# Patch embedding of a vision tower: two more chunks of the first row of patches computed in 28 passes instead of 19

## The chip, the core and the metric

The kernel runs on one NeuronCore of a Trainium2 chip. The metric is the device time of one execution in microseconds (us). The engines are named as the profile names them: PE is TensorE (PEld is its weight load), ACT is ScalarE, DVE is VectorE, POOL is GpSimd, and SP only issues transfers.

## What is computed

The reference is one layer of a vision tower on 128 images of 3 x 224 x 224. Only its first part is touched here, but the second part waits for it:

```
# patches of 28 x 28 pixels x 3 colours, 8 rows of 8 patches in an image
patches = X.reshape(B, 3, 8, 28, 8, 28).transpose(0, 2, 4, 1, 3, 5).reshape(B, 64, 2352)
tokens  = einsum('bpi,hi->bph', patches, W) + b            # 2352 -> 128
tokens  = concatenate([class_token, tokens], axis=1) * pos_embed      # 65 tokens
h = tokens + attention(layernorm(tokens))   # gated attention with a damped moving average
h = h + experts(layernorm(h))               # 8 experts, each takes its 1024 best tokens
```

The attention runs over the 128 images at one token position, so each of the 65 positions can be worked on as soon as its own tokens are there. The experts need all positions.

## The kernel before

**Chunks.** A row of patches (8 of them, all images) is computed in eight chunks of 16 images, so there are 64 chunks, numbered n from 0. Eight of them make one row; the first row is chunks 0 to 7. A chunk is loaded by three transfers into one of three buffers (`RAW`). It has 84 partitions: 28 pixel rows x 3 colours. Each pixel column of the patch is then one pass of PE: a matmul with 84 partitions of pixels against the weights of that column, added up in PSUM. There are 28 columns (`PATCH`), which would be 28 passes.

**Shifted columns.** To save passes the last nine columns (`REST`) can be folded into the 44 partitions that are left over. POOL copies the nine columns of a chunk to a staging buffer `ST` (one of two, by n % 2; line 588, `stage_C`), and two transfers issued by POOL (line 601, `stage_w`) move the two halves of the pixel rows to partitions 84 to 125 beside the first eighteen columns. The first 18 passes then have 126 partitions, one more has 84, and the chunk takes 19 passes (`PASSES`).

**Direct chunks.** A chunk listed in `DIRECT` is not shifted. It takes 28 passes of 84 partitions: nineteen read the copy that ACT makes (line 697, into `XS`), and nine read the staging buffer `ST` itself, with weights that are kept in the tiles `G` and `XR` for a while. PE does both kinds in the same routine (`token_pass`, line 1397). POOL may refill a buffer of `ST` only when its last reader is done. For a shifted chunk that is the pair of transfers, for a direct chunk it is PE:

```
if n - 2 in DIRECT:
    pool.wait_ge(*pe_tok.done(n - 2))
else:
    pool.wait_ge(*extras[n % 2].done(shifted(n - 2)))
```

**Order of the work.** All engines run the same hand-written list of steps, `SLOT`, in which `"C 0 3"` is POOL's staging copy of a chunk (in the first iteration that of chunk 3; `"C 1 3"` is chunk 4), `"C 0 0"` to `"C 0 2"` are ACT's three copies of it, and the other letters are stages of the attention for a group of four token positions (or, for the first group, `CLS`, of the class token alone). In the first iteration the part of the list that matters here reads

```
"S b", "C 0 3", "w 0", "T a", "U b", "C 0 0", "Z b", "P b", "N a", "K 0", "X a", "E a", "C 0 1", "C 0 2", "W 0", "O b", "C 1 3", ...
```

For the class group `a`, `T` is PE's transpose of its tokens (line 1436), then ACT's copy and DVE's statistics (lines 943 and 948, tile `mvA`). `N` is POOL's reciprocal root (lines 510 and 512, tile `rsA`) and then DVE's normalised `X` (line 935). `X` is PE's transpose of it (line 1446). `V` is lines 1456 and 984; `D` and `I` are matmuls with `WmT` (lines 1471 to 1482). In the first iteration PE has the class group alone beside the tokens, and it fills up between the stages with passes: chunk 0 ahead of `T`, chunk 1 behind `T`, chunk 2 behind `X`, chunk 3 behind `V`, and so on (`FILL_CLS`). Each engine is strictly in order, so a step that waits holds all that stands behind it on its engine. When chunk 7 is done DVE adds bias and position (line 955, `tokT`), and the groups of the first row begin.

**Ahead of the first pass** DVE works out small constants (lines 913 to 931); PE, and POOL from chunk 3 on, wait for their end (`consts_done`).

Of the kernel before, what the change touches and what calls it, by code (L numbers as in the profile page):

```python
# [17 lines left out]
def begun(n):  # L18

    return not isinstance(n, int) or n >= 0  # L20
# [15 lines left out]
def vit_tower(nc, x, tok_w, tok_b, cls_token, pos_embed, proj_v_w, proj_v_b, proj_mx_w, proj_mx_b,  # L36
# [44 lines left out]
    CHUNKS = B // CHUNK  # L81
# [7 lines left out]
    with ctx:  # L89
# [278 lines left out]
        AHEAD = 3  # L368
        DIRECT = range(3, CHUNKS)

        def passes_of(n):
            return PATCH if n in DIRECT else PASSES

# [3 lines left out]
        def shifted(n):  # L377

            return len([m for m in range(n % 2, n, 2) if m not in DIRECT])

# [116 lines left out]
        def _(pool):  # L497
# [77 lines left out]
            def stage_C(n, piece):  # L575
# [5 lines left out]
                if begun(n - 2):  # L581
                    if n - 2 in DIRECT:
                        pool.wait_ge(*pe_tok.done(n - 2))
# [7 lines left out]
            def stage_w(n):  # L591

                if n in DIRECT:
                    return
# [744 lines left out]
        def _(pe):  # L1339
# [39 lines left out]
            def token_pass(p):  # L1379
# [4 lines left out]
                if t == 0:  # L1384
                    pe.wait_ge(*copied.done(n))
                    if n in DIRECT:
                        pe.wait_ge(*staged.done(n))
                    else:
                        pe.wait_ge(*extras[n % 2].done(shifted(n)))
                    if k % 4 == 0 and begun(i - 1):  # L1390
                        pe.wait_ge(*dve_K[half].done(i - 1))
                rows = slice(0, KROWS if t < 2 * REST and n not in DIRECT else ROWS)
                if t < PASSES:
# [305 lines left out]
```

## Time and profile before

| | us |
|---|---|
| median of three runs (lowest, highest) | 955.01 (953.62, 955.89) |
| profiled execution, its own time | 960.5 |
| its span in the profile | 958.4 |
| PE busy | 766.0 |
| POOL busy | 477.1 |
| DVE busy | 561.4 |
| ACT busy | 445.5 |

The span is what the profile covers from the first instruction to the last; the time of the same execution is 2.1 us longer. The durations below come from this one execution. The token passes (line 1397) end at about 554 us; what follows is the rest of the attention, the choice of tokens and the experts.

### The profile page before, as it was taken

How to read it: one execution, taken by the hardware profiler on the slowest of the kernel's cores; microseconds unless marked ns; L12 is line 12 of the kernel's file. 1: busy time of each engine (PE TensorE's matmuls, PEld its weight loads, DVE VectorE, ACT ScalarE, POOL GpSimd, SP SyncE). 2: the span in 40 equal slices, each digit the busy share in tenths (PEclk: the TensorE clock that was granted, in tenths of full speed). 3: DMA queues.
4: the chain of work that ended last, by engine and by line, in shares of the span. 5: the costliest groups of instructions: out<-in, count | busy, mean ns of one | idle time of the engine just before them, and what ended most of it. 6: DMA issues, size and time to landing. Idle time of an engine off the chain costs nothing.

```text
span 958.4 us, 13714 instructions
## 1 busy us (share of the span) xinstructions
PE 766.0 (80%) x4819; PEld 595.1 (62%) x4819; DVE 561.4 (59%) x1239; ACT 445.5 (46%) x733; POOL 477.1 (50%) x478
## 2 busy tenths in 40 slices
PE   1799999999999999999999966443167999788771
PEld 1799888878887887888888754131124554444330
DVE  1303687788788778777877865944877433321110
ACT  2553666666756666665676624210550233222220
POOL 2314554555445546455544512441103578887885
PEclk9899999999999999999999996856557899888896
DMA  9977999998898898889889210000101133433432
GB/s 225 211 174 175 214 211 207 212 205 203 198 221 193 204 219 198 195 200 216 193 202 219 76 56 22 11 12 22 11 4 24 29 63 59 64 62 65 67 40 25
DMA packets 135057, 124.71 MB, mean 130 GB/s; under 512 B 17385, under 2 KB 125793, under 8 KB 134861
## 3 DMA queue, kind: packets, MB, share of 16 engines
q1 hardware_dynamic: 113600, 91.27, 41.7%
q0 software_dynamic: 18848, 31.58, 17.4%
q10 hardware_dynamic: 2540, 0.99, 0.5%
q8 instruction: 39, 0.64, 0.3%
q14 instruction: 30, 0.24, 0.1%
HBM read 87.99 MB, written 12.98 MB: 105 GB/s over the span
## 4 chain that ended last, share of the span: by engine, by line
DVE 27%; PE 23%; POOL 22%; issue 16%; ACT 6%; DMA 3%; ACTq 1%; another core or an unknown queue 0%; SPq 0%; DVEq 0%; POOLq 0%
POOL out L641 10%; PE bank L1397 9%; POOL XS L631 6%; DVE Y L993 4%; PE bank L1503 3%; DVE stats L943 3%; DVE XR L935 3%; DVE O L935 3%; DVE QT L1067 3%; ACT XS L844 2%; POOL rsB L512 2%; ACT S L800 2%; PE bank L1488 2%; POOL rsC L512 2%; PE bank L1534 2%
## 5 line engine op out<-in xcount | busy, mean ns | idle before, releaser
L1397 PEld LDWEIGHTS bank<-XS,WT 126*128 126x128 f32 (+1 forms) x2432 | 303.6, 191 | 20.7 <-issue 20.0
L1397 PE MATMUL bank<-XS,WT 126*128 126x128 f32 (+1 forms) x2432 | 310.5, 283 | 6.1 <-issue 6.1
L697 ACT ACTIVATE XS<-XS 84x1152 f32<-84x1152 f32 (+1 forms) x192 | 184.4, 1032 | 0.0
L588 POOL COPY XS<-XS 84x1152 f32<-84x1152 f32 x64 | 91.3, 1427 | 62.9 <-PE bank L1397 32.1
L641 POOL DMA_INDIRECT out<-XS x64 | 105.4, 1647 | 27.2 <-issue 18.7
L631 POOL DMA_INDIRECT XS<-token_rows,XS x64 | 65.4, 1022 | 54.8 <-DVE XS L1270 35.9
L993 DVE TENSOR_TENSOR_SCAN Y<-qdec,XT 128x512 f32<-128x512 f32 (+1 forms) x68 | 78.3, 1173 | 2.5 <-ACT XT L733 2.5
L873 ACT ACTIVATE XS<-bank,VT 128x512 f32<-128x512 f32 x64 | 43.8, 688 | 70.4 <-PE bank L1615 70.4
L601 POOL DMA_DIRECT2D XS<-XS x118 | 66.4, 565 | 17.3 <-POOL XS L588 17.3
L1615 PE MATMUL bank<-XS 128*128 128x512 f32 x128 | 68.8, 687 | 1.1 <-ACT XS L733 0.8
L999 DVE SCALAR_TENSOR_TENSOR ET<-Y,ema_c,ET 128x512 f32<-128x512 f32 (+1 forms) x68 | 62.7, 922 | 1.8
L1625 PE MATMUL bank<-XS 128*128 128x512 f32 x128 | 57.5, 592 | 0.0
L510 POOL TENSOR_SCALAR rsA<-mvA 128x4 f32<-128x4 f32 (+1 forms) x17 | 3.9, 232 | 95.5 <-DVE mvA L948 95.5
L733 ACT ACTIVATE XS<-bank 128x512 f32<-128x512 f32 x16 | 9.6, 597 | 89.7 <-PE bank L1606 83.2
L562 POOL TENSOR_TENSOR QT<-QT,XT 128x512 f32<-128x512 f32 (+1 forms) x17 | 23.3, 1372 | 55.0 <-ACT QT L814 55.0
L1286 DVE TENSOR_SCALAR XS<-bank,VT 128x512 f32<-128x512 f32 x16 | 12.0, 750 | 63.1 <-PE bank L1625 48.5
L1615 PEld LDWEIGHTS bank<-XS 128*128 128x128 f32 x128 | 27.6, 228 | 31.7 <-issue 31.6
L935 DVE TENSOR_SCALAR XR<-O,mvC,rsC 128x128 f32<-128x128 f32 x65 | 42.5, 918 | 8.0 <-POOL rsC L512 7.9
L510 POOL TENSOR_SCALAR rsB<-mvB 128x4 f32<-128x4 f32 (+1 forms) x17 | 15.1, 889 | 60.6 <-DVE mvB L948 60.6
L955 DVE SCALAR_TENSOR_TENSOR tokT<-bank,VT 128x512 f32<-128x512 f32 x16 | 17.9, 1118 | 46.1 <-PE bank L1397 46.1
L1625 PEld LDWEIGHTS bank<-XS 128*128 128x128 f32 x128 | 24.1, 190 | 29.7 <-issue 29.5
L1054 DVE SCALAR_TENSOR_TENSOR G<-bank,VT,GT 128x512 f32<-128x512 f32 (+1 forms) x34 | 24.7, 727 | 28.2 <-PE bank L1503 27.5
(243 smaller groups left out, 1332.1 us busy)
## 6 DMA issues: line engine op xcount, KB each, us to landing
XS<-in_x SPq DMA_DIRECT2D x192, 392.0 KB
XS<-XS POOLq DMA_DIRECT2D x118, 189.0 KB, 7.5
out<-O SPq DMA_DIRECT2D x16, 256.0 KB, 9.7
token_rows<-XR SPq DMA_DIRECT2D x16, 256.0 KB, 8.6
XS<-in_L_ffn_W SPq DMA_DIRECT2D x16, 256.0 KB
XS<-in_L_tok_W SPq DMA_DIRECT2D x1, 1176.0 KB, 9.3
XS<-token_rows,XS POOLq DMA_INDIRECT x65, 3.7
out<-XS POOLq DMA_INDIRECT x64
```

Of the source, the lines that this page charges most:

```text
L588: pool.tensor_copy(ST[0:ROWS, n % 2, :, :, :].rearrange("p m j r -> p m r j"), px[:, :, :, PASSES:PATCH])\
L601: pool.dma_start(area(slice(ROWS, KROWS), k // 4, a, m0, m0 + CCOL // 2), ST[EXTRA * a:EXTRA * a + EXTRA, n % 2, :, :, :]).then_inc(extras ...
L631: pool.indirect_dma_start(out=XG[h][:, k, :], out_offset=None, in_=rows_d, in_offset=bass.IndirectOffsetOnAxis(ap=IDX[:, e, k:k + 1], axis ...
L641: pool.indirect_dma_start(out=out_flat, in_=OW[:, e % 2, k, :], in_offset=None, out_offset=bass.IndirectOffsetOnAxis(ap=IDX[:, e, k:k + 1] ...
L697: ins = act.activation(area(slice(0, ROWS), k // 4, piece, m0, m0 + CCOL // 2).rearrange("p m j r -> p m r j"), px[:, :, :, REST * piece:m ...
L873: act.activation(HT[:, h, f, :], bank[3 + f][:, :], ACT.Gelu, bias=VT[:, ds(R_B1 + FC * e + f, 1)]).then_inc(act_hid.sem, 1)
L935: last = dve.tensor_scalar(dst(t), src(t), mv[:, gr.parity, t, 0:1], rs[:, gr.parity, t:t + 1], ALU.subtract, ALU.mult)
L993: dve.tensor_tensor_scan(Y[:, h % 2, 0:n], qdec[:, h, 0:n], XT[:, p, 0:n], 0.0, ALU.mult, ALU.add)\
L999: dve.scalar_tensor_tensor(out=ET[:, gr.parity, 0:n], in0=Y[:, h % 2, 0:n], scalar=ema_c[:, h:h + 1], in1=ET[:, gr.parity, 0:n], op0=ALU.m ...
L1397: ins = pe.matmul(TOK[half][:, c0:c0 + CCOL], weights, pixels, start=(t == 0), stop=(t == passes_of(n) - 1))
L1615: pe.matmul(bank[3 + f][:, :], W1s[:, h, 128 * f:128 * f + 128], XGT[:, half, :], start=True, stop=True).then_inc(pe_hid.sem, 1)
L1625: last = pe.matmul(bank[7][:, :], W2s[:, h, f, :], HT[:, half, f, :], start=(f == 0), stop=(f == FC - 1))
```

## The change

`DIRECT`, the chunks that are not shifted, is chunks 3 to 7 before and chunks 1 to 7 with the change. Nothing else differs.

```
-        DIRECT = range(3, CHUNKS)
+        DIRECT = range(1, CHUNKS)

         def passes_of(n):
             return PATCH if n in DIRECT else PASSES
```

On PE, behind the transpose of the class tokens (L1436), the program reads as follows against before. `WT` holds the weights of the first nineteen columns, `G` and `XR` those of the last nine, and 128x128 is the shape of the result.

```order
 L1436 MATMUL bank<-ident,tokT 128x128
 L1397 MATMUL bank<-XS,WT 128x128 x19
+L1397 MATMUL bank<-XS,G 128x128 x8
+L1397 MATMUL bank<-XS,XR 128x128
 L1446 MATMUL bank<-ident,X 128x128
 L1397 MATMUL bank<-XS,WT 128x128 x19
+L1397 MATMUL bank<-XS,G 128x128 x8
+L1397 MATMUL bank<-XS,XR 128x128
 L1456 MATMUL bank<-WvT,XT 128x128 x2
 L1397 MATMUL bank<-XS,WT 128x128 x19
```

Nine passes are added ahead of `X` (chunk 1) and nine behind it (chunk 2). On POOL, from the staging copy of chunk 1 on, this stood before, with the semaphores that each waits for (`load` is a chunk's arrival, `extras` the two shifting transfers, `pe_tok` PE's last pass of a chunk, `dve_T` the statistics):

```order
L588 COPY XS<-XS 84x64x2x9 [waits load1]
L601 DMA XS<-XS 42x1152 [waits staged]
L601 DMA XS<-XS 42x1152
L588 COPY XS<-XS 84x64x2x9 [waits load2,extras0]
L601 DMA XS<-XS 42x1152 [waits staged]
L601 DMA XS<-XS 42x1152
L588 COPY XS<-XS 84x64x2x9 [waits consts_done,load0,extras1]
L510 TENSOR_SCALAR rsA<-mvA 128x1 [waits dve_T]
L512 TENSOR_TENSOR rsA<-rsA,neghalf 128x1 [waits pool_N]
```

And this stands there now, from the same copy on:

```order
L588 COPY XS<-XS 84x64x2x9 [waits load1]
L588 COPY XS<-XS 84x64x2x9 [waits load2,extras0]
L588 COPY XS<-XS 84x64x2x9 [waits consts_done,load0,pe_tok]
L510 TENSOR_SCALAR rsA<-mvA 128x1 [waits dve_T]
L512 TENSOR_TENSOR rsA<-rsA,neghalf 128x1 [waits pool_N]
L522 TENSOR_TENSOR H<-H,lnb 128x128 [waits dve_N]
L588 COPY XS<-XS 84x64x2x9 [waits load1,pe_tok]
```

Four transfers are gone. The copy of chunk 3, which stands directly ahead of the class group's reciprocal root, waits for PE's last pass of chunk 1 where it waited for the shifting of chunk 1; the next one, of chunk 4, waits for PE's last pass of chunk 2. DVE, ACT and SP have the same instructions in the same order as before.

## Rows read from the trace of the kernel before

**Rows 1.** The page: the span, and the granted clock in 40 slices

```profile
span 958.4 us, 13714 instructions
PEclk9899999999999999999999996856557899888896
```

**Rows 2.** Chain that ended last, 24 to 125 us: start, us, what

```profile
33.30 7.02 PE bank L1397 x38
...
40.43 4.55 PE bank L1397 x38
...
50.09 6.70 PE bank L1397 x56
...
57.24 6.70 PE bank L1397 x56
...
64.39 20.11 PE bank L1397 x168
...
84.52 1.12 DVE tokT L955
```

**Rows 3.** Waits of PE from 90 to 530 us: in total, times, longest

```profile
PE bank L1520 <- DVE X L1071: 5.7, 13, 0.7
...
PE bank L1534 <- ACT X L733: 0.4, 1, 0.4
```

**Rows 4.** Timeline at chunk 1: start, us, engine, line [idle before <-releaser]

```profile
40.27 4.71 PE L1397 MATMUL bank<-XS,WT 126*128 126x128 f32 x38
...
41.28 0.18 DVE L948 BATCH_NORM_AGGREGATE mvA<-stats 128x2 f32<-128x6 f32 x1
41.69 0.24 POOL L510 TENSOR_SCALAR rsA<-mvA 128x1 f32<-128x1 f32 x1 [3.62 <-DVE mvA L948]
42.01 0.59 POOL L512 TENSOR_TENSOR rsA<-rsA,neghalf 128x1 f32<-128x1 f32 x1
42.63 0.35 DVE L935 TENSOR_SCALAR X<-H,mvA,rsA 128x128 f32<-128x128 f32 x1 [1.17 <-POOL rsA L512]
...
44.82 0.27 PE L1446 MATMUL bank<-ident,X 128*128 128x128 f32 x1
```

**Rows 5.** Timeline at chunk 5, a direct one

```profile
64.22 4.70 PE L1397 MATMUL bank<-XS,WT 84*128 84x128 f32 x38
...
70.68 0.40 PE L1397 MATMUL bank<-XS,XR 84*128 84x128 f32 x2
...
71.25 1.33 POOL L588 COPY XS<-XS 84x1152 f32<-84x1152 f32 x1 [5.83 <-PE bank L1397]
```

**Rows 6.** Timeline of DVE and POOL ahead of the first pass

```profile
28.88 1.23 DVE L917 COPY qdec<-ema_t 128x2048 f32<-128x2048 f32 x1
28.92 2.34 POOL L588 COPY XS<-XS 84x1152 f32<-84x1152 f32 x1 [3.99 <-DMA XS<-in_x]
...
30.29 0.97 DVE L919 TENSOR_TENSOR ema_t<-ema_t,ema_in 128x4 f32<-128x4 f32 x1
31.30 0.16 DVE L920 TENSOR_TENSOR ema_c<-ema_t,ema_in 128x4 f32<-128x4 f32 x1
```

**Rows 7.** Timeline of PE: three transposes with PE's idle time ahead

```profile
560.60 0.68 PE L1495 MATMUL bank<-ident,S 128*128 128x128 f32 x2 [3.69 <-DVE S L1043]
...
605.73 0.44 PE L1520 MATMUL bank<-ident,X 128*128 128x128 f32 x2 [2.67 <-DVE X L1071]
...
654.47 0.66 PE L1520 MATMUL bank<-ident,X 128*128 128x128 f32 x4 [3.58 <-DVE X L1071]
```

**Rows 8.** Stretches: busy time of five engines, then PEclk, DMA share, GB/s

```profile
33.00:38.00 5.00, 4.70 (x22) 4.73 (x23) 0.14 (x2) 0.00 (x0) 1.23 (x1) 0.50 0.97 220
...
560.00:565.00 5.00, 4.13 (x22) 3.73 (x23) 2.02 (x6) 1.92 (x3) 2.04 (x2) 0.66 0.02 5
602.00:606.00 4.00, 1.33 (x7) 0.85 (x6) 3.93 (x6) 0.05 (x1) 1.42 (x1) 1.00 0.00 0
650.00:655.00 5.00, 1.42 (x7) 0.48 (x5) 1.38 (x2) 0.69 (x1) 1.26 (x1) 1.00 0.00 0
```

## The prediction, made before the changed kernel ran

> **What bounds the kernel now.** I read the page first, for the span and the clock: PE's granted clock is at 8 or 9 tenths from the second slice on to about 550 us [rows 1]. Then the chain that ended last, from 24 to 125 us. The reader is to see that from 33.30 to 84.5 us it never leaves PE: chunk 0 (38 instructions, two to a pass), chunks 1 and 2 at 4.55 us each, then the direct chunks at 6.70 us each, with only the few matmuls of the class group between; behind chunk 7 it goes to DVE, which makes the tokens for the first groups [rows 2]. So the first row of patches is a queue of passes on PE, and all that follows waits for its end. Then the waits of PE from 90 to 530 us, to see whether a later row could give back what the first one loses: there are five rows, the longest 5.7 us in 13 waits, the smallest 0.4, and none of them is for a load or for a copy of a chunk [rows 3]. From then on, too, PE or what it hands to DVE and gets back sets the time, and nothing waits for the memory. A delay of the first row arrives at the end undiminished.
>
> **The added passes.** A chunk of 19 passes, 18 of them with 126 partitions, takes 4.55 us for 38 instructions, 119.7 ns each; a direct chunk takes 6.70 us for 56 instructions with 84 partitions, 119.6 ns each [rows 2]. Time goes by the pass and not by the partitions, so nine passes more cost 6.70 - 4.55 = 2.15 us a chunk, and two chunks **4.3 us**. Neither chunk had a wait ahead of it that they could fill: each starts as the one before it ends [rows 2, 4].
>
> **The wait that moves to POOL.** The staging copy of chunk 3 now waits for PE's last pass of chunk 1, and the class group's reciprocal root stands behind it in POOL's queue; behind that come DVE's `X` and, on PE, the transpose L1446, which stands directly behind chunk 1. Before, the root ran from 41.69 to 42.60 and `X` was there at 42.98, while PE was busy with chunk 1 until 44.8: 1.8 us to spare [rows 4]. Now, step by step:
> - Chunk 1 starts at 40.27 [rows 4]. A direct chunk ends 6.86 us after its start (64.22 to 70.68 + 0.40 [rows 5]), so it ends at 47.13. POOL's copy follows 0.17 us behind such an end (71.08 to 71.25) and takes 1.33 [rows 5]: 47.30 to 48.63.
> - The two root instructions took 0.91 us from start to end (41.69 to 42.60), DVE's `X` 0.38 with its handover (to 42.98) [rows 4]: 49.54, then 49.92. With some 0.05 us to PE, by the size of the handover to DVE, the transpose starts at 49.97.
> - PE would have come to it at 44.82 + 2.15 = 46.97. So it stands idle for **3.0 us**.
>
> That is exposed to its full length, since PE is in order and chunk 2 stands behind the transpose. Half a chunk's passes left to do there would have covered it.
>
> The next such wait, of chunk 4's copy on the end of chunk 2, costs nothing: the class group's `X` is then past, and nothing that PE needs soon stands behind the copy. Chunk 2 ends at about 56.9, the copy at 58.3, and PE wants chunk 4's staged columns only after chunk 3, 6.7 us behind chunk 2 [rows 2]; the cover is some 6 us. Chunk 3's own staged columns are there at 48.6 and are wanted after 57. ACT's copies of chunks 3 to 5 stand behind ACT's copy of the class group's transpose, and so come some 5 us later; PE wants the first of them over 7 us after that transpose, one chunk and a little more, and there are two pieces of about 1 us to do. The loads that hang on these copies shift with the stream. I cost all of these at nothing.
>
> **What is taken away.** Four transfers and their issue on POOL. PE did not wait for them. There is one way in which they could matter. Ahead of the first pass DVE's chain of small operations is on the path. L919, 0.97 us, has as many elements as L920, 0.16 us, and it ends at 31.26, exactly where POOL's copy of chunk 2 ends, which itself took 2.34 us where 1.33 is usual, while L917 ran [rows 5, 6]. So the two engines hold each other up there. That copy was waiting for its load; without the shifting of chunk 1 beside it, the load may land sooner and the copy be out of the way. Bounds: 0 if the load lands as before, 0.97 - 0.16 = 0.8 us if the collision is gone. I take **0.3**, nearer the lower end, since the two transfers of chunk 1 are only a part of what is under way in that stretch beside the loads, and a copy only a little earlier would hold up L917 in its turn.
> The Trainium skill, SBUF — State Buffer, section "Who interferes with whom", says that DVE and GpSimd lock a shared pair of ports for a whole instruction and the loser waits. The equal ends at 31.26 agree with it. By that rule alone, with the copy started before L917 and done before L919, the whole 0.8 us would come back.
>
> **The clock after the wait.** PE's clock is at 1.2 GHz until 38 us and at its full 2.4 GHz when the wait comes [rows 1, 8]. A wait of 3.0 us might cost it. The trace has three like it that began at full clock. Idle for 2.67 us at 603 to 606, the clock stayed at 1.00; idle for 3.58 us to 654.47, it was at 1.00 still at 655; idle for 3.69 us to 560.60, it fell to 1.2 GHz [rows 7, 8]. In the last the mean of 0.66 over 5 us means 5 x (1 - 0.66) / 0.5 = 3.4 us at the lower level. What that costs is seen at chunk 0: 7.02 us against 4.55 for the same 38 instructions, 2.5 us lost over the 5 us and a little at 0.50 from 33 on [rows 2, 8], so 0.47 us for each us, and 3.4 us would cost 1.6. The bounds are 0 and 1.6. I take **0**, since 3.0 us lies next to 2.67 and below 3.58, which both held.
> The Trainium skill, TensorE: Matmul & The Clock Gate, section "HAM oscillation — how this bites in real kernels", warns that an array which waits between bursts falls back to its half rate and pays the way up each time. By that the sum would be the one with 1.6 in it.
>
> **Sum.** 4.3 + 3.0 - 0.3 + 0 = 7.0 us. The profiled execution would go from its own 960.5 to 967.5 (span 965.4). It was 5.5 us above the median of the runs, 955.0, so I put the same difference on the median: **962.0 us**.
>
> **The rivals.**
> - *The clock falls after the wait.* 7.0 + 1.6 = 8.6: 963.6. For it: the 3.69 us wait, and that its outcome may differ between executions. Against it: the two that held.
> - *The wait is not there*, because something lets the root through earlier, or `X` isn't needed where I think. Then 4.3 - 0.3 = 4.0: 959.0. Against it: the order on POOL and PE, which leaves no other way.
> - *Not slower: later rows give it back.* If the loads set the pace of the later rows, a longer first row would let them run ahead, and the rows after it would close up. It would need PE to wait for chunks in the later rows by more than 5.1 us in sum, to bring 7.0 under 1.9. PE's waits there add up to 16 us, but all are for results of DVE and ACT that come from PE's own earlier work [rows 3]. It would give 955 to 957.
> - *Another queue is late too*, say ACT's three copies behind the class group's transpose: one more wait of 2 to 4 us, 964 to 966. The cover counted above speaks against it.
>
> **How the numbers follow.** The forecast has a chance of 0.52, the clock's fall 0.29, the added passes alone 0.07, another late queue 0.06, and no slowdown 0.06, of which 0.02 faster. What a measurement of this kernel can tell from no change is about 0.2%, 1.9 us; its three runs lie within 2.3 us. All cases but one are beyond that bound on the slow side: slower 0.94, same 0.04, faster 0.02. The range is to hold the forecast and the clock's fall with the prologue's 0 to 0.8 us (961.5 to 963.9), and the scatter of the runs, 1.2 us to a side; that is 960.3 to 965.1, rounded outward a little toward the two neighbouring cases: 960.0 to 965.8.
>
> **What the changed profile would show.** L1397 with 36 instructions more. Behind L1436, 56 of them in one run of about 6.9 us. Then PE idle by 3 us ahead of L1446, released by DVE's `X` (L935), at about 50 us. POOL's L588 of chunk 3 released by PE at about 47, and rsA directly behind it. DVE's `tokT` for the second half at about 91.5 where it was 84.52 [rows 2]. Then the same periods as before. PEclk at 1.00 in the stretch from 47 to 57 if the clock holds, lower if the first rival has it. If L919 takes 0.16 us and the first pass starts before 33.3, the prologue gave something back. The prediction is wrong if PE goes from chunk 1 to L1446 with no idle time, or if a wait for a chunk turns up on PE between 50 and 91 us, or if the time between `tokT` and the end has changed by more than 1 us.

## The result, and the profile after

The changed kernel takes 994.43 us (993.24 to 996.05) where the one before takes 954.63 on the same chip: a ratio of 1.0417, with a 95% interval of 1.0387 to 1.0447, 39.8 us slower. The prediction was 962.0, in a range of 960.0 to 965.8. The sign was right and the size was not: some 33 us are missing from the sum.

The page of the changed kernel shows where to look. In the row of the granted clock the slices two to five, of 24.8 us each, are at 8, 5, 5 and 5 tenths where before they stood at 8 or 9 [rows 1], and PE is busy all the same:

```profile
span 993.5 us, 13782 instructions
...
PE   1699999999999999999999995725228899878771
...
PEclk9855589999999999999999998775555798889896
```

The chain that ended last (start, us, what) answers to [rows 2]:

```profile
33.39 7.44 PE bank L1397 x38
...
40.94 6.72 PE bank L1397 x56
...
50.99 11.95 PE bank L1397 x56
...
63.79 11.95 PE bank L1397 x56
...
89.39 35.85 PE bank L1397 x168
...
125.27 1.13 DVE tokT L955
```

Chunk 1 takes 6.72 us for its 28 passes, as forecast. Chunk 2, behind the wait, takes 11.95 for the same 56 instructions, and so do all chunks up to the seventh (35.85 for three). Between chunks 1 and 2 is the wait, in the timeline of the changed kernel, which answers to [rows 4, 5]:

```profile
41.80 0.18 DVE L948 BATCH_NORM_AGGREGATE mvA<-stats 128x2 f32<-128x6 f32 x1
...
47.25 0.40 PE L1397 MATMUL bank<-XS,XR 84*128 84x128 f32 x2
47.82 1.26 POOL L588 COPY XS<-XS 84x1152 f32<-84x1152 f32 x1 [16.47 <-PE bank L1397]
49.17 0.24 POOL L510 TENSOR_SCALAR rsA<-mvA 128x1 f32<-128x1 f32 x1
49.50 0.58 POOL L512 TENSOR_TENSOR rsA<-rsA,neghalf 128x1 f32<-128x1 f32 x1
50.12 0.35 DVE L935 TENSOR_SCALAR X<-H,mvA,rsA 128x128 f32<-128x128 f32 x1 [8.14 <-POOL rsA L512]
...
50.52 0.47 PE L1446 MATMUL bank<-ident,X 128*128 128x128 f32 x1 [2.87 <-DVE X L935]
```

The statistics are ready at 41.98 and the root starts at 49.17, behind the copy. PE stands idle for 2.87 us. The stretches of the changed kernel (length, then busy time of PE, PEld, DVE, ACT and POOL, the granted clock, DMA share, GB/s) show the clock at this place, in the middle of what follows, and at the start of the second row of patches:

```profile
48.00:49.00 1.00, 0.00 (x0) 0.00 (x0) 0.00 (x0) 0.00 (x0) 1.00 (x1) 1.00 0.00 0
49.00:50.00 1.00, 0.00 (x0) 0.00 (x0) 0.00 (x0) 0.00 (x0) 0.82 (x3) 0.85 0.00 0
50.00:51.00 1.00, 0.48 (x2) 0.49 (x3) 0.35 (x1) 0.00 (x0) 0.53 (x2) 0.50 0.00 0
...
100.00:125.00 25.00, 25.00 (x119) 25.00 (x118) 0.00 (x0) 0.00 (x0) 3.70 (x4) 0.50 0.50 118
...
130.00:131.00 1.00, 1.00 (x6) 1.00 (x6) 0.05 (x1) 0.00 (x0) 0.92 (x2) 0.50 0.05 14
131.00:132.00 1.00, 1.00 (x8) 1.00 (x7) 0.68 (x3) 0.00 (x0) 0.28 (x1) 0.69 0.00 0
132.00:133.00 1.00, 1.00 (x11) 1.00 (x10) 0.43 (x2) 0.00 (x0) 0.49 (x1) 1.00 0.00 0
```

The clock falls from 2.4 to 1.2 GHz at about 49.7 us, while PE is idle, and stays there until 131.6, although PE is busy from 50.5 to 125 without a break, as one stretch over all of it shows:

```profile
50.00:125.00 75.00, 74.48 (x349) 74.49 (x350) 4.86 (x12) 18.20 (x26) 8.11 (x9) 0.50 0.44 102
```

It comes back some 4 us into chunk 8, the first shifted chunk since chunk 0 (the four transposes of the new tokens, with 128 partitions, stand just before it, at 126.5). That is nearly the whole of what is missing. By `tokT` of the second half the changed kernel is 125.27 - 84.52 [rows 2] = 40.75 us late, and this adds up: 4.3 for the added passes (6.72 + 6.70 - 2 x 4.55), 2.9 for the wait, 0.4 for chunk 0 (7.44 against 7.02), and for the clock six chunks at 11.95 - 6.70 = 5.25, which is 31.5, with the class group's few matmuls between them 1.6 more. Together 40.7.

The two profiled spans differ by less, 35.1 us, so from `tokT` to the end the changed kernel is 5.6 us shorter in its profile; the prediction had named more than 1 us there as a sign of being wrong. The changed one is still 42 us behind when the choice of tokens ends (726.10 and 768.10 us for the first matmuls of L1588), and 36 behind at the first stores of the experts (760.39 and 796.40, L641). Between the two the chain of the execution profiled before has a wait that the other has not:

```profile
738.54 3.81 another core or an unknown queue
```

It is in the executions profiled of several other kernels too, whatever the change. That it explains the 5.5 us by which the one before was above its median is not shown: the kernels with the root first and with the warm start, below, have this wait in their profiled executions as well, and these took 963.70 and 958.61 us, no more than their medians. Where the 5.5 us lie stays open. The comparison goes by the medians, 39.8 apart, which agree with the 40.75 at `tokT` to 1 us.

### The profile page after: what moved, and what is told of

Same layout as the page of the kernel before. It is cut to its first block, busy times and chain, and to the rows that moved or that the text cites. A ratio compares the mean times of both kernels' runs of the same rounds, so it can differ in the third digit from the quotient of the medians.

```text
span 993.5 us, 13782 instructions
## 1 busy us (share of the span) xinstructions
PE 803.2 (81%) x4855; PEld 632.0 (64%) x4855; DVE 560.6 (56%) x1239; ACT 445.0 (45%) x733; POOL 472.8 (48%) x474
## 4 chain that ended last, share of the span: by engine, by line
PE 27%; DVE 26%; POOL 21%; issue 15%; ACT 6%; DMA 4%; ACTq 1%; SPq 0%; DVEq 0%; POOLq 0%
PE bank L1397 12%; POOL out L641 8%; POOL XS L631 6%; DVE Y L993 4%; PE bank L1503 3%; DVE stats L943 3%; DVE XR L935 3%; DVE O L935 3%; DVE QT L1067 2%; ACT XS L844 2%; POOL rsB L512 2%; ACT S L800 2%; PE bank L1488 2%; POOL rsC L512 2%; PE bank L1534 2%
## 5 line engine op out<-in xcount | busy, mean ns | idle before, releaser
L1397 PEld LDWEIGHTS bank<-XS,WT 126*128 126x128 f32 (+1 forms) x2432 | 327.6, 205 | 20.3 <-issue 19.6
L1397 PE MATMUL bank<-XS,WT 126*128 126x128 f32 (+1 forms) x2432 | 334.4, 297 | 6.0 <-DVE stats L931 6.0
L641 POOL DMA_INDIRECT out<-XS x64 | 104.5, 1632 | 25.4 <-issue 18.3
L601 POOL DMA_DIRECT2D XS<-XS x114 | 64.2, 566 | 16.8 <-POOL XS L588 16.7
```

The costliest lines, as they stand in the source:

```text
L601: pool.dma_start(area(slice(ROWS, KROWS), k // 4, a, m0, m0 + CCOL // 2), ST[EXTRA * a:EXTRA * a + EXTRA, n % 2, :, :, :]).then_inc(extras ...
L641: pool.indirect_dma_start(out=out_flat, in_=OW[:, e % 2, k, :], in_offset=None, out_offset=bass.IndirectOffsetOnAxis(ap=IDX[:, e, k:k + 1] ...
L1397: ins = pe.matmul(TOK[half][:, c0:c0 + CCOL], weights, pixels, start=(t == 0), stop=(t == passes_of(n) - 1))
```

## The experiments

Theory A, formed from this profile: the wait lets PE's clock fall, and the direct passes, with 84 partitions, never bring it back, whereas the shifted ones, with 126, do. The first four kernels vary the order on POOL and which chunks are direct. Each time is given beside the kernel before on the same chip, and the ratio with its interval. Absolute times in the expectations count from 955; what is compared is the distance from the kernel before. The stretches have the same columns as above.

**The root ahead of the copy.** The 36 extra instructions stay; only the wait is taken away, by POOL's order in the first iteration:

```
-            for entry in SLOT:
+            order = SLOT
+            if i == 0 and u == 0:
+                order = [e for e in SLOT if e not in ("C 0 3", "w 0")]
+                at = order.index("N a") + 1
+                order = order[:at] + ["C 0 3", "w 0"] + order[at:]
+            for entry in order:
```

> The changed kernel, but in the first iteration POOL has the class group's reciprocal root ahead of the staging copy of chunk 3, so that nothing on PE waits for that copy. Theory A (the 3 us wait ahead of L1446 lets PE's clock fall to 1.2 GHz, and the direct passes of 84 partitions behind it never bring it back): no wait of PE over 1 us between 40 and 85 us, the clock at 1.00 up to the end of chunk 7, and only the 4.3 us of added passes: 959. Rival B (it is the longer succession of 84-partition passes itself that brings the clock down): the clock falls in the first row all the same, 985 to 995.

Measured: 964.06 against 958.61, ratio 1.0052 (1.0036 to 1.0069), 5.0 us by the ratio where 4.3 was expected. The stretch that holds most of the direct chunks:

```profile
60.00:85.00 25.00, 25.00 (x212) 25.00 (x211) 1.18 (x1) 10.38 (x15) 5.30 (x4) 1.00 0.72 164
```

The clock is at 1.00, and in 25 us PE gets through 212 instructions where at the low clock it was 119. With the wait gone, 35 of the 39.8 us are gone. Rival B falls.

**Chunk 1 shifted, chunks 2 to 7 direct.**

```
-        DIRECT = range(1, CHUNKS)
+        DIRECT = range(2, CHUNKS)
```

> Direct chunks are 2 to 7; chunk 1 is shifted as before the change. The copy of chunk 3 then waits for transfers that have long landed, and the root is not held. Theory A: no wait, no fall of the clock, 9 more passes, 2.15 us: 957. Rival B: with 6 chunks of 84-partition passes in succession instead of 5 the clock falls near the end of the row at the latest, 960 or more.

Measured: 959.76 against 958.61, ratio 1.0002 (0.9985 to 1.0018). The clock is at 1.00 from 41 to 85 us, so Rival B falls here too. The 2.15 us do not show in the times: the interval ends at 1.7 us. They do show in the trace, where `tokT` starts at 87.80, 3.3 us later than before, 1.1 of it already there when chunk 1 starts. Why the times have less is open.

**Chunk 2 shifted, chunks 1 and 3 to 7 direct.** The wait is there, but what stands behind it is a chunk with 126 partitions.

```
-        DIRECT = range(1, CHUNKS)
+        DIRECT = (1, *range(3, CHUNKS))
```

> Direct chunks are 1 and 3 to 7; chunk 2, which stands right behind the wait, is shifted, 18 of its 19 passes with 126 partitions. Theory A: the wait of 3 us and the fall of the clock are there, but chunk 2 brings the clock back within some 5 us, and chunks 3 to 7 run at 1.00: 2.15 for chunk 1, 2.9 for the wait, about 2.4 for the clock: 962. Rival C (once fallen, the clock stays down while PE is busy without a break, whatever the passes are): low to about 120 us as in the changed kernel, 988 to 992.

Measured: 966.05 against 958.61, ratio 1.0085 (1.0064 to 1.0105). In its stretches the clock is down behind the wait and back within chunk 2:

```profile
47.00:50.00 3.00, 0.12 (x3) 0.01 (x1) 0.35 (x1) 0.00 (x0) 2.09 (x3) 1.00 0.03 9
50.00:55.00 5.00, 5.00 (x29) 5.00 (x30) 3.69 (x8) 4.61 (x7) 1.72 (x2) 0.66 0.08 13
55.00:60.00 5.00, 5.00 (x44) 5.00 (x43) 0.52 (x2) 3.33 (x6) 0.00 (x0) 1.00 0.95 230
```

5 x (1 - 0.66) / 0.5 = 3.4 us low, just the time at the low clock that the prediction had reckoned with, and chunk 2 takes 6.04 us instead of 4.55, 1.5 more, where the prediction had 1.6. The wait is the same as in the changed kernel (2.88 us), and so is the fall; so the 30 us between the two come from what stands behind the fall. Rival C falls.

**All eight chunks direct.**

```
-        DIRECT = range(1, CHUNKS)
+        DIRECT = range(0, CHUNKS)
```

> All eight chunks of the first row are direct, chunk 0 too, whose 126-partition passes stood behind the clock's rise at 38 us. Theory A: the clock, at 1.2 GHz at the first pass, never rises in the first row, and all eight chunks take about 12 us each: the row ends about 11 us later than with the change, 1005. Rival C (a steady stream of any passes raises the clock after some 5 us, it is the fall behind a wait that sticks): the clock rises in chunk 0 and falls at the wait, 9 passes more than the changed kernel, 996 to 998.

Measured: 1009.35 against 958.61, ratio 1.0529 (1.0511 to 1.0546). One stretch holds the whole first row:

```profile
31.00:133.00 102.00, 99.12 (x464) 98.83 (x464) 5.41 (x15) 19.65 (x28) 11.62 (x12) 0.50 0.42 98
```

But for the wait of 2.9 us ahead of L1446, which is there too, PE is busy for all of the 102 us, and the clock is at 0.50 throughout. In the kernel before it rose in chunk 0; without that chunk's 126-partition passes it never does in this row. Theory A had 50 us above the kernel before, and it is 50.7.

**What stands behind the wait.** Now only the passes behind L1446 change. Twenty passes of chunk 0 are repeated there, in one kernel with their 126 partitions, in the other with the first 84; they write a part of PSUM that chunk 2 overwrites.

```
+            def extra(n):
+                for t in range(n):
+                    pe.matmul(TOK[0][:, 2 * CCOL:3 * CCOL], WT[0:KROWS, t % 18, :],
+                              area(slice(0, KROWS), 0, t % 18 // REST, 0, CCOL // 2)[:, :, t % 18 % REST, :], start=True, stop=True)
...
                 last.then_inc(pe_X.sem, 1)
+                if gr is CLS:
+                    extra(20)
```

With 126 partitions (`KROWS`):

> The changed kernel with 20 extra passes on PE between the transpose L1446 and chunk 2: they repeat chunk 0's passes with 126 partitions into a part of PSUM that chunk 2 then overwrites, and leave the result as it is. Theory A (passes of 126 partitions bring the clock back, those of 84 do not): the clock rises within some 5 us behind the wait, and chunks 2 to 7 run at full clock; the 20 passes cost 7 to 7.5 us, the wait 3, the added passes 4.3: 15 us above the kernel before, 24 below the changed one, although it does more. Rival C (what is down stays down while PE is busy): the changed kernel plus 8.5, 48 above the kernel before.

With 84 (`ROWS` in both places):

> The same 20 extra passes at the same place, with the first 84 of the 126 partitions, the same instructions and shapes else. Theory A: the clock stays at 1.2 GHz to the end of the first row: 0.426 us a pass, 8.5 us above the changed kernel, 48 above the kernel before. Rival D (it is the extra stretch of work that lets the clock rise, whatever its partitions): as the run with 126 partitions, 15 above the kernel before.

Measured: with 126 partitions 974.47 against 960.57, ratio 1.0135 (1.0106 to 1.0165); with 84 partitions 1009.20 against the same 960.57, ratio 1.0498 (1.0468 to 1.0527). The direct chunks in the first, and then in the second:

```profile
60.00:100.00 40.00, 40.00 (x338) 40.00 (x337) 1.69 (x3) 10.40 (x15) 7.72 (x7) 1.00 0.62 145
```

```profile
60.00:130.00 70.00, 70.00 (x330) 70.00 (x329) 1.74 (x3) 10.43 (x15) 7.61 (x7) 0.50 0.37 87
```

The rise comes behind 55 us in the first, while the twenty passes run (they end at 58.7), and not at all in the second:

```profile
55.00:60.00 5.00, 5.00 (x36) 5.00 (x35) 0.00 (x0) 4.60 (x7) 0.00 (x0) 0.80 0.80 188
```

```profile
55.00:60.00 5.00, 5.00 (x25) 5.00 (x25) 0.25 (x1) 4.83 (x7) 0.00 (x0) 0.50 0.75 176
```

The two programs have the same instructions in the same order and differ in one number. They lie 34.7 us apart, 13.9 and 48.6 above the kernel before, on either side of the changed kernel's 39.8: twenty useless passes with 126 partitions make it faster by some 26 us. Rival D falls. No number between 84 and 126 was tried, so where the line lies, and whether it is the count or which of the 128 partitions are used, is open.

**Zeros.** The same twenty, with the identity on both sides:

```
+                    pe.matmul(TOK[0][:, 2 * CCOL:3 * CCOL], ident[:, :], ident[:, :], start=True, stop=True)
```

> The changed kernel with 20 extra matmuls behind the transpose L1446, as in the two runs before with 126 and with 84 partitions, but now 128 partitions of the identity against the identity, of which nearly every element is zero; they write a part of PSUM that chunk 2 overwrites. Theory A, by partitions: the clock rises as behind the 126-partition passes, 14 us above the kernel before. Rival G, by what the numbers are (zeros don't count as work): the clock stays low, 48 above.

Measured: 968.43 against 954.85, ratio 1.0148 (1.0124 to 1.0171), 13.6 us, as with the 126-partition passes. The direct chunks:

```profile
60.00:99.00 39.00, 39.00 (x329) 39.00 (x328) 1.68 (x3) 10.38 (x15) 7.74 (x7) 1.00 0.62 146
```

So nearly all the numbers in the partitions can be zero here, and the clock rises all the same. Rival G falls.

**The wait filled.** Ahead of L1446 PE gets 12 passes of 84 partitions; POOL and DVE are as late as before.

```
             def stage_X(gr):
+                if gr is CLS:
+                    extra(12)
                 pe.wait_ge(*dve_N.done(gr.g))
```

> The changed kernel with 12 extra passes of 84 partitions on PE ahead of the transpose L1446, where it waits for 2.9 us; the wait for the root on POOL keeps its length, but PE works in it (12 passes of 0.24 us are 2.9). Theory A: no idle time, so the clock never falls: 4.3 for the added passes and 2.9 for the wait, 7.2 above the kernel before, which is what the prediction had without the clock. Rival E (the fall comes from something else than idle time at this place, say the passes of chunk 1 with 84 partitions so early): the clock falls at about 50 us all the same, 40 above.

Measured: 966.84 against 960.57, ratio 1.0064 (1.0043 to 1.0085). In its timeline `X` comes at the same distance behind the copy, and PE is at work until it does:

```profile
47.12 3.04 PE L1425 MATMUL bank<-XS,WT 84*128 84x128 f32 x24
47.45 1.31 POOL L588 COPY XS<-XS 84x1152 f32<-84x1152 f32 x1 [17.16 <-PE bank L1397]
...
50.20 0.33 PE L1453 MATMUL bank<-ident,X 128*128 128x128 f32 x1
```

The clock is at 1.00 from 47 to 85 us. The 6.3 us between the medians (4.1 to 8.1 by the interval) agree with the 7.2 expected and with the prediction's sum, 7.0. Rival E falls: it is PE's idle time, and not the late root, that costs the clock.

The same profile has another fall, behind the first row:

```profile
85.00:125.00 40.00, 37.31 (x264) 33.96 (x263) 18.37 (x40) 19.46 (x29) 20.46 (x26) 0.96 0.80 180
```

PE waits 1.08 us up to 93.38 and 0.81 us up to 94.82; the clock falls at about 95.7, while PE is at work, and is back at about 99.1, within chunk 8's passes of 126 partitions. That is 3.4 us low. So the clock can fall behind short waits too, and with such passes behind them it is soon back. It need not fall: the kernel of the warm start, below, has waits of 1.08 and 0.83 us at this place and stays at 1.00.

**Warm ahead of the first pass.** In the kernel before, PE gets 22 matmuls in its idle time ahead of chunk 0:

```
+            for t in range(22):
+                pe.matmul(bank[1][:, 0:128], ident[:, :], ident[:, :], start=True, stop=True)
             pe.wait_ge(*pro_evac.done(11))
             pe.wait_ge(*consts_done.done(0))
```

> The kernel before, with 22 matmuls of 128 partitions (the identity with itself, into a part of PSUM that is overwritten) on PE ahead of the first pass, where PE is idle from about 27.4 to 33.3 us. Theory A: the clock does not fall ahead of chunk 0, which takes 4.55 us instead of 7.0: 2.4 faster than the kernel before. Rival F: chunk 1 or the class group then waits for DVE or for the shifting instead, and the gain is 0 to 1.

Measured: 958.63 against 960.57, ratio 0.9980 (0.9967 to 0.9994): the only version of this study that is faster than the kernel before, and by little. Chunk 0 takes 4.62 us (33.81 to 38.43), so the clock gives back what Theory A had; but the first pass starts 0.5 us later than before, and 1.9 us is left of the 2.4. The first stretches are at 1.00 where [rows 8] has 0.50:

```profile
27.00:33.00 6.00, 5.22 (x45) 5.03 (x45) 4.35 (x13) 5.16 (x12) 2.93 (x3) 1.00 0.96 200
33.00:38.00 5.00, 4.19 (x35) 4.22 (x36) 0.57 (x4) 0.00 (x0) 1.30 (x1) 1.00 0.98 219
```

**All direct, but warm.** The kernel with all eight chunks direct, with those 22 matmuls and with the root ahead of the copy:

> All eight chunks direct as in the run that was 50.7 us slower, with two things added: 22 matmuls of the identity on PE in its idle time ahead of the first pass, and the root ahead of the copy of chunk 3. No pass of the first row has over 84 partitions. Theory A: the clock is held at 1.00 from the first pass to the end of chunk 7, since it never falls: 3 x 2.15 = 6.5 for the passes, less 2.4 for the clock of chunk 0: 4 above the kernel before. Rival H (passes of 84 partitions can't hold the clock from the start either, they need 126-partition passes ahead of them): 45 to 50 above.

Measured: 958.40 against 954.85, ratio 1.0045 (1.0017 to 1.0073). The first row:

```profile
33.00:90.00 57.00, 55.39 (x463) 55.02 (x463) 8.75 (x21) 21.34 (x32) 14.28 (x15) 1.00 0.70 165
```

The same 224 passes of the first row as in the kernel that was 50.7 us slower now cost 3.6 (1.6 to 7.0), with the two things added together; neither was tried alone. Nothing with more than 84 partitions stands between 33 us and the end of the row but the class group's few matmuls, and the clock holds. Rival H falls: these passes keep the clock that they find.

**The change the other way.** Chunk 3 shifted as well, alone and with the 22 matmuls:

```
-        DIRECT = range(3, CHUNKS)
+        DIRECT = range(4, CHUNKS)
```

> The change the other way: direct chunks 4 to 7, chunk 3 shifted too. By the passes, 2.15 us below the kernel before. Rival: the shifting of chunk 3 or the loads come late, PE waits ahead of chunk 3, and the gain is gone (0, or slower if such a wait costs the clock before the direct chunks).

> Direct chunks 4 to 7 and the 22 matmuls ahead of the first pass. If both gains add up: 2.15 + 1.9 = 4 below the kernel before. Rival: the loads, which already held ACT up by 2.3 us in the run with the 22 matmuls alone, are the bound of the first row, and it is no faster than that run, 2 below.

Measured: 956.78 against 954.85, ratio 1.0020 (1.0000 to 1.0039), and with the matmuls 975.78 against 954.85, ratio 1.0220 (1.0198 to 1.0243). By the passes both should have been faster. The first is no faster, 0 to 3.7 us slower by its interval, its rival's case in time, and the second outdoes its own: two changes of which each should take 2 us away add 21 together. The second one's timeline and stretches:

```profile
52.17 2.80 ACT L697 ACTIVATE XS<-XS 84x1152 f32<-84x1152 f32 x3 [3.58 <-DMA XS<-in_x]
...
55.22 0.49 PE L1473 MATMUL bank<-ET,WmT 128*128 128x128 f32 x2 [2.15 <-ACT ET L762]
```

```profile
53.00:55.20 2.20, 0.07 (x1) 0.00 (x0) 1.14 (x1) 2.17 (x4) 0.69 (x1) 1.00 0.98 199
55.20:57.00 1.80, 1.78 (x15) 1.78 (x16) 0.00 (x0) 0.62 (x2) 0.00 (x0) 1.00 0.98 222
57.00:58.00 1.00, 1.00 (x8) 1.00 (x7) 0.00 (x0) 0.00 (x0) 0.00 (x0) 0.54 0.99 204
58.00:100.00 42.00, 42.00 (x199) 42.00 (x199) 0.00 (x0) 9.64 (x13) 4.97 (x5) 0.50 0.58 132
```

PE is now so early that ACT waits 3.58 us for the load of a chunk; the class group's relu (L762) stands behind those copies, and PE waits 2.15 us for it. The clock is still up at 57.0, 1.8 us after PE is at work again, falls then, and four direct chunks run low, which is the 21 us (4 x 5.25). That this wait causes the fall is argued from its place; no run takes it away. With chunk 3 shifted alone, PE's wait for the same relu is 1.2 us in the profiled execution and the clock holds. There PE waits for a relu behind a load, and not for chunk 3 itself as the rival had it. One of the four executions took 975.77 us at a mean granted clock of 0.875 against 0.896 to 0.899 in the others; there is no trace of it, and what it shows is open.

## Why the prediction was wrong

- **What bounds the kernel**: right. PE's queue of the first row sets the time, and its loss arrives at the end: 40.75 us at `tokT` of the first row, 39.8 in the medians.
- **The added passes**, 4.3 us: right. The direct chunk took 6.72 us at full clock, and the kernel without the wait is 5.0 us slower (3.5 to 6.6).
- **The wait that moves to POOL**, 3.0 us: right, in its place, its order and its size, 2.87. The steps (copy 47.30, root 48.63, transpose 49.97) came 0.5 us later, for chunk 0 had taken 0.4 more. The covers counted for the other waits held: no other wait turned up on PE.
- **What is taken away**, 0.3 us: nothing came back. The two rows that answer to [rows 6] are unchanged, the copy still starts with the landing of its load, just behind L917, and L919 still ends with it:

```profile
29.02 2.33 POOL L588 COPY XS<-XS 84x1152 f32<-84x1152 f32 x1 [5.19 <-DMA XS<-in_x]
...
30.38 0.97 DVE L919 TENSOR_TENSOR ema_t<-ema_t,ema_in 128x4 f32<-128x4 f32 x1
```

- **The clock after the wait** is the step that failed, twice over. I took 0 because waits of 2.67 and 3.58 us had held the clock and only one of 3.69 had lost it [rows 7, 8]; here 2.87 us lost it. The trace before had more to say than those three rows. The two waits that held were followed only to their ends; PE then worked for 0.66 us and was idle again, and the clock fell at 608.4 and 656.2, 2.7 and 1.8 us after them. And it had fallen once with PE at work, at 587.9, behind waits of 1.50 and 0.69 us. The first row below is the end of the longer of these two; the rest are stretches:

```profile
584.87 0.66 PE L1527 MATMUL bank<-ident,XR 128*128 128x128 f32 x4 [1.50 <-DVE XR L935]
...
587.50:588.00 0.50, 0.50 (x6) 0.50 (x6) 0.00 (x0) 0.01 (x1) 0.00 (x0) 0.95 0.00 0
588.00:588.50 0.50, 0.50 (x5) 0.50 (x4) 0.01 (x1) 0.00 (x0) 0.00 (x0) 0.50 0.00 0
...
608.00:608.50 0.50, 0.00 (x0) 0.00 (x0) 0.37 (x2) 0.00 (x0) 0.00 (x0) 0.93 0.00 0
...
656.00:656.50 0.50, 0.00 (x0) 0.00 (x0) 0.50 (x4) 0.00 (x0) 0.00 (x0) 0.72 0.00 0
```

The length of a wait alone did not decide, and "held" was more than those rows showed. The larger error was the upper bound, 1.6 us, for the time at the low clock. It was worked out as 3.4 us at the low clock, from a fall that dense work with 128 partitions ended, and priced by chunk 0, whose passes have 126. I did not ask what would end the fall *here*. In [rows 2] direct chunks run at full clock for 34 us, and I read from that, and from equal times for 84 and 126 partitions, that the two kinds were alike. In that trace no direct pass ever stands at the low clock: it could show that they hold the clock, and could not show that they raise it. The fall cost 33 us, 20 times the bound: 82 us at the low clock, from 49.7 to 131.6, where the bound had 3.4. With a shifted chunk behind the wait it cost 1.5 us, as the bound had it.

The Trainium skill, TensorE: Matmul & The Clock Gate, section "HAM oscillation — how this bites in real kernels", had warned of a fall behind a wait, and the trace agrees with it, though the waits of its example are of about 3 to 5 us and this one is 2.87. Its section "What's actually happening" says that the throttled state is the default and that activity releases it; the changed kernel has 74.5 us of activity without a gap and stays at 1.2 GHz, so for passes of 84 partitions the measurement decides against that sentence as it stands.

The chances had the sign at 0.94. They had no case for a fall that lasts, so that the range, with all its cases, ended 27 us below the lowest execution.

## What to carry to other kernels

Before a wait is put ahead of PE, look at what stands behind it: if that is work with fewer partitions (here 84 of the 128), a lost clock may not come back until the next work that uses nearly all of them, and the price is about half the speed of everything up to there, and not of some microseconds. A bound taken from another place in the trace holds only if the instructions that end the state are the same, and a wait is to be followed in the trace some microseconds past its end before it is said to have held the clock. Where such a wait can't be avoided, a few matmuls in it, or twenty full-width ones behind it, cost less than the fall. And fewer passes or an earlier start can be the dearer choice, when PE then runs into a wait that it did not have.

## What the runs showed of the hardware

- PE at 1.2 GHz, fed without a break with fp32 passes of 84 partitions and 128 columns, stayed there for 75 us in the changed kernel, and with all chunks direct for 102 us, there with one wait of 2.9 us in them (in both apart from the few matmuls between them). The same passes, with PE at 2.4 GHz when they began, ran at 2.4 GHz from 33 us to the end of the row at 86.6 with all chunks direct and the warm start.
- Twenty passes with 126 partitions, or with 128 of an identity, brought it back at this place (at about 57 us in the first case, some 5.5 us after they began); twenty with 84 did not.
- A wait of 2.87 us let the clock fall, 2.0 us into the idle time; with PE at work in its place it stayed up. A wait of 2.15 us was followed by a fall 1.9 us after its end, waits of 1.08 and 0.81 us by one 0.9 us after the second had ended, and waits of 1.50 and 0.69 us by one 1.7 us after the second had ended. At the end of one of 3.58 us [rows 7] the clock was still up, and it fell 1.8 us later. What besides the length decides is not settled here.
